# Three graph convolutions at the start of a fused convolution, attention and expert kernel

## The chip, the cores and the metric

The kernel runs on one core of a Trainium2 chip. The time is the device time in microseconds of one execution; three runs of the kernel before took 1002.51 to 1003.75 us, median 1003.73. TensorE is the matrix engine, VectorE (DVE), ScalarE (ACT) and GpSimd (POOL) work on rows, and SyncE (SP) issues the transfers.

## The reference

`x` is 16 x 256 x 16 x 16 (sample, node or channel, feature, time). Three blocks follow one another:

```python
x = x + graph_conv(group_norm(x))        # attention over time (16x16) and over nodes (256x256), 3 Chebyshev
                                         # filters, a convolution over time, residual, relu, norm over time
t = tokens(x)                            # 16 x 256 tokens of 256 channels
t = t + linear_attention(layer_norm(t))  # causal, 16 heads, elu + 1
t = t + moe(layer_norm(t))               # 16 experts of 64, 4 chosen within 2 of 4 groups, and a shared one of 512
```

The convolution of a sample needs only that sample, and so do attention and experts. All is fp32; the large products of attention and experts are made of three products of high and low halves (`mm3`, L501 to L503), and each weight matrix is split into such halves once, at the start.

## The kernel before, in words

The 16 samples go in 8 pairs. Each pair passes five chains of steps: `conv` (22 steps: gn, xg, xT0 ... tc1), `tail` (xb, z1, z2, z3: the norm over time and the sum with x), `attn` (tok0 ... wo1), `route` (tk0 ... cb: layer norm and the choice of experts) and `ffn` (for j from 0 to 11 the steps gu, h, dn, w, on TensorE the gate and up products, the spread product of routed chunks and the down product).

The order of all steps is written out in three texts, OPENING, BODY (used for five turns) and CLOSING. A word such as `1:p2` is step p2 of pair 1, and `+2` puts in the next two steps of the ffn chain, whose own order is fixed. `program()` makes one list of them, and `run` (L504 and on) walks that list on every engine: each engine issues only its own part of a step, in the order of the list. No engine goes ahead of the list; the engines are tied by semaphores, and each chain counts its own results (`Signal`). Up to the first word with a plus, OPENING holds the convolutions of pairs 0 and 1, attention and routing of pair 0, most of the convolution of pair 2 and the first steps of pair 1's attention. In BODY the ffn of pair p, the attention of pair p+1 and the convolution of pair p+2 are laid beside one another.

Products of conv, attn and route go to four PSUM banks in a ring: a tile takes the bank of the fourth tile before it in the order and waits for that one's last reader (`wait_bank`). The steps Y0, Y1, S.., rd take four banks each and p2 two. The ffn has g_ps, u_ps and d_ps, and num serves values and routing.

The scratch of a convolution is a "room". There are two: room 0, for pair 0, lies in the memory that attention uses later (`shared`), and all other pairs use room 1, one after another. Therefore, from pair 2 on, gn and xg of a pair wait for the pair before it (o1, xb1, n30, n31, vs1).

The weights come in 15 pieces of 384 KB (the first is smaller), loaded by SP behind all inputs with no wait (L569) into `raw`, a buffer whose place in memory is that of the low halves (`wqkv_l`, `gate_l`, `up_l`, `down_l`): the high half is written elsewhere by ScalarE (`split`, L661), and then the low half over the raw piece by VectorE (L813). Both splits hang on steps by two tables, HIGH_AT and LOW_AT, such as `"1:st1": 6`, six low splits behind pair 1's st1. The first gu step waits for 6 low halves of weights behind the attention's, gu of j = 2 for all gate and up pieces.

A pair's x is loaded as soon as xb1 of the pair before is done (`prefetch`). POOL does xb, half of z1 and z3, and the low half of the hidden values (L647) in each w step.

Of the lines that are named below: L1218 is gn's product, L1225 the transposes xT, L1237 M, L1191 Y, L1288 sp (with vs_s), L1305 o, L1177 S, L1206 V, L1336 tok and tk, L945 the product with the Chebyshev filters, L950 to L974 the tail, L1031 the causal mask.

Of the kernel before, what the change touches and what calls it, by code (L numbers as in the profile page):

```python
# [54 lines left out]
class Signal:  # L55

    def __init__(self, sem, names, first=None):
# [316 lines left out]

# [1184 lines left out]
```

## Time and profile before

| | us |
|---|---|
| median of three runs | 1003.73 |
| profiled execution, its own time | 1005.99 |
| its span, first to last instruction | 1004.2 |
| TensorE busy | 941.5 (94%) |
| VectorE busy | 606.8 (60%) |
| ScalarE busy | 426.0 (42%) |
| GpSimd busy | 210.2 (21%) |
| mean granted TensorE clock | 0.952 |

The first feed-forward product starts at 188.43 us; pair 0's transposes at the start of attention (tok0) stand at 95.04, its first scores (S00) at 132.92 and its output product (wo0) at 163.96.

### The profile page before, as it was taken

How to read it: one execution, taken by the hardware profiler on the slowest of the kernel's cores; microseconds unless marked ns; L12 is line 12 of the kernel's file. 1: busy time of each engine (PE TensorE's matmuls, PEld its weight loads, DVE VectorE, ACT ScalarE, POOL GpSimd, SP SyncE). 2: the span in 40 equal slices, each digit the busy share in tenths (PEclk: the TensorE clock that was granted, in tenths of full speed). 3: DMA queues.
4: the chain of work that ended last, by engine and by line, in shares of the span. 5: the costliest groups of instructions: out<-in, count | busy, mean ns of one | idle time of the engine just before them, and what ended most of it. 6: DMA issues, size and time to landing. Idle time of an engine off the chain costs nothing.

```text
span 1004.2 us, 20050 instructions
## 1 busy us (share of the span) xinstructions
PE 941.5 (94%) x8208; PEld 832.8 (83%) x8208; DVE 606.8 (60%) x1630; ACT 426.0 (42%) x808; POOL 210.2 (21%) x184
## 2 busy tenths in 40 slices
PE   4797779999999999999999999999999999999997
...
PEclk9689757999999999999999999999999999999999
...
DMA packets 14378, 17.78 MB, mean 18 GB/s; under 512 B 1072, under 2 KB 12720, under 8 KB 14288
## 3 DMA queue, kind: packets, MB, share of 16 engines
...
## 4 chain that ended last, share of the span: by engine, by line
PE 86%; DVE 6%; ACT 6%; issue 1%; POOL 0%; DMA 0%; POOLq 0%; SPq 0%; DVEq 0%; ACTq 0%
PE ring L1305 9%; PE g_ps L501 5%; PE d_ps L501 5%; PE d_ps L503 4%; PE d_ps L502 4%; PE g_ps L503 4%; PE g_ps L502 4%; PE u_ps L501 4%; PE u_ps L502 4%; PE u_ps L503 4%; PE ring L1177 4%; PE num L1206 3%; PE ring L1288 3%; PE ring L501 3%; PE ring L503 3%; PE ring L502 3%
## 5 line engine op out<-in xcount | busy, mean ns | idle before, releaser
L647 POOL TENSOR_TENSOR hl<-hb,hh 128x512 fp32r<-128x512 f32 x96 | 127.2, 1325 | 494.4 <-ACT hh L791 494.4
L1145 DVE TENSOR_TENSOR hb<-sl,u_ps 128x512 f32<-128x512 f32 x88 | 60.2, 684 | 99.9 <-PE u_ps L503 48.4
L791 ACT ACTIVATE hh<-hb 128x512 fp32r<-128x512 f32 x96 | 60.8, 633 | 140.1 <-DVE hb L1149 119.7
L501 PE MATMUL d_ps<-hh,down_h 128*128 128x256 f32 x384 | 114.9, 299 | 1.9 <-POOL hl L647 1.9
L501 PE MATMUL g_ps<-normed_h,gate_h 128*128 128x256 f32 x352 | 109.0, 310 | 3.6 <-DVE scb L1061 3.5
L503 PE MATMUL d_ps<-hh,down_l 128*128 128x256 f32 x384 | 107.5, 280 | 0.0
L502 PE MATMUL d_ps<-hl,down_h 128*128 128x256 f32 x384 | 107.4, 280 | 0.0
L503 PE MATMUL g_ps<-normed_h,gate_l 128*128 128x256 f32 x352 | 100.4, 285 | 0.0
L501 PE MATMUL u_ps<-normed_h,up_h 128*128 128x256 f32 x352 | 100.1, 284 | 0.0
L502 PE MATMUL g_ps<-normed_l,gate_h 128*128 128x256 f32 x352 | 100.1, 284 | 0.0
L502 PE MATMUL u_ps<-normed_l,up_h 128*128 128x256 f32 x352 | 100.1, 284 | 0.0
L503 PE MATMUL u_ps<-normed_h,up_l 128*128 128x256 f32 x352 | 99.9, 284 | 0.0
L1031 DVE TENSOR_TENSOR shared<-ring,constants 128x512 f32<-128x512 f32 x128 | 79.2, 680 | 23.5 <-PE ring L1177 23.5
L788 ACT ACTIVATE sl<-g_ps 128x512 f32<-128x512 f32 x88 | 52.6, 598 | 74.5 <-PE g_ps L503 74.2
L501 PEld LDWEIGHTS d_ps<-hh,down_h 128*128 128x128 f32 x384 | 72.2, 188 | 11.0 <-issue 5.6
L501 PEld LDWEIGHTS g_ps<-normed_h,gate_h 128*128 128x128 f32 x352 | 67.2, 191 | 14.6 <-issue 11.8
L502 PEld LDWEIGHTS d_ps<-hl,down_h 128*128 128x128 f32 x384 | 72.3, 188 | 1.7 <-issue 1.7
L503 PEld LDWEIGHTS d_ps<-hh,down_l 128*128 128x128 f32 x384 | 72.3, 188 | 0.0
L502 PEld LDWEIGHTS g_ps<-normed_l,gate_h 128*128 128x128 f32 x352 | 67.5, 192 | 0.8 <-issue 0.5
L503 PEld LDWEIGHTS g_ps<-normed_h,gate_l 128*128 128x128 f32 x352 | 67.6, 192 | 0.0
L501 PEld LDWEIGHTS u_ps<-normed_h,up_h 128*128 128x128 f32 x352 | 67.4, 191 | 0.0
L502 PEld LDWEIGHTS u_ps<-normed_l,up_h 128*128 128x128 f32 x352 | 67.3, 191 | 0.0
...
## 6 DMA issues: line engine op xcount, KB each, us to landing
out_x<-kept SPq DMA_DIRECT2D x16, 256.0 KB, 2.1
x_s<-in_x SPq DMA_DIRECT2D x14, 256.0 KB, 3.0
raw_weights<-in_gateT SPq DMA_DIRECT2D x4, 384.0 KB, 9.2
raw_weights<-in_upT SPq DMA_DIRECT2D x4, 384.0 KB, 10.1
raw_weights<-in_down SPq DMA_DIRECT2D x4, 384.0 KB, 12.6
cheb_s<-in_cheb SPq DMA_DIRECT2D x3, 256.0 KB, 4.8
raw_weights<-in_wqkvT SPq DMA_DIRECT2D x2, 384.0 KB, 6.9
shared<-in_x SPq DMA_DIRECT2D x2, 256.0 KB, 2.9
```

What stands on the lines that cost most here:

```text
L501: eng.matmul(ps, wh, xh, start=start, stop=False, **how)
L502: eng.matmul(ps, wh, xl, start=False, stop=False, **how)
L503: return eng.matmul(ps, wl, xh, start=False, stop=stop, **how)
L647: pool.tensor_tensor(hl[:, j % 2, :], hb, hh[:, j % 2, :].bitcast(F32), ALU.subtract).then_inc(*ffn_pool.mark(p, f"lo{j}"))
L788: act.activation(sl, gate_up(p, j)[0][:, :], ACT.Silu).then_inc(*ffn_act.mark(p, f"si{j}"))
L791: act.activation(hh[:, j % 2, :], hb, ACT.Copy).then_inc(*ffn_act.mark(p, f"hi{j}"))
L1031: dve.tensor_tensor(p_s[:, j, :].rearrange("p (h l) -> p h l", h=4), tile(p, n)[:, :].rearrange("p (h l) -> p h l", h=4), const_at("causal ...
L1145: dve.tensor_tensor(hb, sl, gate_up(p, j)[1][:, :], ALU.mult).then_inc(*ffn_dve.mark(p, f"h{j}"))
L1177: last = pe.matmul(tile(p, n)[:, 2 * c * P:(2 * c + 2) * P], k_f[rows, c, cols], q_eo[rows, :, c, cols], start=True, stop=True, tile_posit ...
L1206: last = pe.matmul(num[rows, c * L + lc * P:c * L + lc * P + P], v_s[:, b, lc, 4 * c + j, 16 * odd:16 * odd + 32], p_s[:, j, (2 * c + odd) ...
L1288: last = pe.matmul(t[:, kc * N:(kc + 1) * N], vs_s[:, jc, kc * P:(kc + 1) * P], g.th[:, b, jc, :], start=(jc == 0), stop=(jc == 1))
L1305: last = pe.matmul(t[:, c * N:(c + 1) * N], g.y_s[b][:, m, c, k], g.a_s[:, k, m, :], start=(k == 0 and m == 0 and c == 0), stop=(k == 2 an ...
```

## The change

There are three rooms in place of two. Pair 0 keeps room 0, a new room 1 serves pair 1 and lies in `raw`, in the place of gate (second row block), up and down weights, with its small fields in `sl` and `hb`; pairs from 2 on use the room of their own. So pair 2 doesn't wait for pair 1. Its x is loaded right behind pair 1's, ahead of all weights of the convolution.

Because room 1 lies where ten of the pieces are loaded, only five pieces are loaded from the start (the spread rows, wqkv twice, gate's first row block twice). SP then waits for n30 and n31 of pair 1, the end of its tail, before the other ten. The order of pieces changes with that.

The splits become steps of the order (`high0` to `high14`, `low1` to `low14`), and so do 24 fillers, `hot0` to `hot23`, each one matmul of the identity with 256 columns of constants into g_ps, whose result nothing reads. All of the fillers stand ahead of the first ffn step. OPENING is new: gn and xg of all three pairs first, then the three convolutions in turn, with 1:o1, 1:tc0, 1:tc1, pair 1's tail and 2:sp1 to 2:o1 beside attention and routing of pair 0. High5 and low5, the first of the ten late pieces, stand at 0:wo0 and 0:wo1; low7, for which the first gu step now waits, stands behind 1:nrm; high12 to 14 and low10 to 14 stand behind 0:gu0. The steps ahead of 0:gu0 are the same as before but for 1:xl1, which goes behind it, and 0:r1 and 2:xb, which come ahead. BODY is ordered anew with the same steps and the same 50 ffn steps a turn. CLOSING is unchanged.

The order, and the end of `program()`'s input (the lines with a minus are the old order):

```diff
 CHAINS["ffn"] = ffn_steps()
+CHAINS["warm"] = [f"hot{i}" for i in range(24)]
+CHAINS["high"] = [f"high{i}" for i in range(15)]
+CHAINS["low"] = [f"low{i}" for i in range(1, 15)]
+ONCE = ("warm", "high", "low")
+ROOMS = 3
 FIRST = {"conv": "gn", "tail": "xb", "attn": "tok0", "route": "tk0"}
 AHEAD = {"conv": 1, "tail": 1, "attn": 0, "route": 0}
 TURNS = (2, PAIRS - 2)
 
 OPENING = """
-    0:gn 0:xg 1:gn 1:xg 0:xT0 0:M 1:xT0 0:xT1 1:M 0:Y0 0:prod 1:xT1 0:xb 0:Epre 1:Y0 0:Eexp 1:prod 0:Erep 0:lr 1:Epre
-    0:p2 1:Eexp 0:sp0 1:Erep 0:rv0 0:sp1 1:lr 0:st0 0:rv1 0:Y1 1:p2 0:st1 0:o0 0:o1 1:sp0 0:tc0 1:rv0 1:sp1 1:st0
-    0:tc1 1:rv1 0:z1 1:Y1 0:z2 1:st1 1:o0 1:o1 0:z3 1:tc0 1:tc1 1:xb 0:tok0 0:tok1 1:z1 0:nrm 2:gn 0:xl0 2:xg 0:xl1
-    1:z2 2:xT0 0:k0 2:M 2:xT1 0:k1 0:v1 0:q0 0:v0 0:kt 0:q1 1:z3 2:Y0 2:prod 0:dent 0:kv 2:Epre 2:Eexp 0:rd 0:S00
-    2:Erep 0:V00 0:S01 2:lr 0:at0 0:V01 0:S10 2:p2 0:V10 0:S11 2:sp0 2:rv0 0:V11 0:at1 2:sp1 2:st0 0:wo0 0:wo1 2:rv1
-    2:Y1 0:tk0 0:tk1 0:nrm2 2:st1 2:o0 0:xn0 0:xn1 1:tok0 1:tok1 1:nrm 2:o1 0:lg 1:xl0 1:xl1 +1 0:r1 0:r2 1:k0 1:k1 +1
-    1:v1 1:q0 1:v0 0:r3 2:tc0 +1 1:kt 1:q1 +1 0:silu 0:r4 +2 2:tc1 2:xb 1:dent 0:cb +1 1:kv +2 1:rd +2 1:S00 +1 1:V00
-    0:exp +3 1:S01 +3 2:z1 +1 1:at0 1:V01 1:S10 +4 1:V10 1:S11 +1 1:V11 +1 1:at1 +3 2:z2 1:wo0 +2 1:wo1 +2 1:tk0 1:tk1
-    +5 1:nrm2 2:z3 +3 1:xn0 1:xn1 +6 1:exp +1
+    0:gn 0:high0 0:hot0 0:xg 1:gn 2:gn 1:xg 0:hot1 2:xg 0:xT0 0:hot2 1:xT0 0:M 0:xT1 0:hot3 0:xb 0:Y0 0:high1 0:prod
+    1:M 2:xT0 0:high2 0:hot4 1:xT1 0:hot5 0:Epre 0:Eexp 1:Y0 0:Erep 1:prod 2:M 0:lr 2:xT1 0:low1 0:hot6 0:p2 1:Epre
+    1:Eexp 0:hot7 2:Y0 0:hot8 0:hot9 0:sp0 1:Erep 0:high3 0:rv0 1:lr 0:sp1 0:hot10 2:prod 0:st0 0:hot11 0:rv1 1:p2
+    0:low2 0:hot12 0:Y1 0:st1 2:Epre 0:o0 0:high4 2:Eexp 1:sp0 1:rv0 0:o1 1:sp1 1:st0 0:tc0 2:Erep 0:tc1 1:rv1 2:lr
+    0:hot13 0:hot14 0:z1 0:z2 1:Y1 2:p2 1:st1 0:z3 1:o0 2:sp0 0:hot15 0:tok0 0:tok1 0:nrm 2:rv0 1:o1 0:xl0 0:xl1
+    0:low3 2:sp1 2:st0 0:k0 0:k1 0:v1 0:q0 0:v0 0:kt 0:q1 1:tc0 2:rv1 1:xb 0:hot16 0:dent 0:kv 0:hot17 0:rd 0:S00
+    1:tc1 0:V00 1:z1 0:S01 0:at0 0:hot18 0:V01 0:S10 1:z2 0:V10 0:S11 0:hot19 0:V11 1:z3 0:low4 0:at1 2:Y1 0:wo0
+    0:low5 0:wo1 0:hot20 0:high5 0:hot21 0:high6 0:hot22 0:tk0 0:tk1 0:hot23 0:low6 0:nrm2 2:st1 0:high7 2:o0 0:xn0
+    1:tok0 0:xn1 1:tok1 0:high8 1:nrm 0:low7 0:low8 0:high9 2:o1 0:lg 2:xb 0:r1 0:high10 0:high11 0:low9 1:xl0 +1
+    0:low10 0:r2 0:high12 1:xl1 0:low11 +1 2:tc0 +1 0:low12 2:tc1 0:high13 0:r3 0:low13 1:k0 1:k1 0:silu 0:high14 1:v1
+    +2 0:r4 +1 1:q0 +1 1:v0 1:kt 1:q1 0:cb 0:low14 +1 1:dent 1:kv +1 1:rd +2 1:S00 +2 1:V00 2:z1 +2 1:S01 +1 1:at0 +1
+    1:V01 +2 1:S10 +1 1:V10 +7 1:S11 +3 1:V11 2:z2 +3 1:at1 +2 0:exp 1:wo0 +1 2:z3 1:wo1 +2 1:tk0 +2 1:tk1 +2 1:nrm2
+    +4 1:xn0 1:xn1 +1 1:exp
 """
 
 BODY = """
-    tok0 tok1 +1 lg +1 nrm gn xl0 xg +1 xl1 +1 xT0 r1 M xT1 +1 k0 +1 k1 v1 r2 +2 r3 Y0 +1 q0 v0 kt q1 prod silu r4 +2
-    Epre dent cb kv +1 rd +2 Eexp S00 +2 Erep +1 lr +3 p2 +2 sp0 rv0 sp1 +1 st0 V00 +2 rv1 Y1 +3 xb S01 +1 st1 +1 at0
-    +1 o0 +1 o1 V01 +1 S10 +1 tc0 +1 tc1 V10 z1 S11 +1 V11 +2 at1 +1 z2 +1 wo0 +1 wo1 +2 tk0 tk1 +5 nrm2 z3 +1 xn0 xn1
-    exp +1
+    tok0 tok1 +1 lg +1 nrm gn xl0 xg +1 xl1 +1 r1 xT0 M +1 k0 k1 +1 r2 v1 xT1 r3 +2 Y0 q0 v0 kt q1 silu +1 r4 +1 prod
+    +1 cb dent kv +1 Epre +1 rd +2 Eexp Erep +1 lr +2 S00 +2 p2 +2 sp0 rv0 sp1 +1 st0 V00 +1 rv1 +2 Y1 +1 S01 +3 st1
+    at0 o0 xb +1 V01 S10 +1 o1 +1 tc0 tc1 z1 +1 V10 +1 S11 +1 V11 +3 at1 z2 +1 wo0 wo1 +3 tk0 tk1 +4 nrm2 +1 z3 +1 xn0
+    xn1 +1 exp
 """
...
```

Rooms, pieces and the loads:

```diff
         rooms = [conv_room(shared[:, 0:3072], shared[:, 3072:6144], shared[:, 6144:7168], shared[:, 7168:7680], shared[:, 2816:3008]),
+                 conv_room(raw[:, 3072:6144], raw[:, 6144:9216], raw[:, 9216:10240], sl, hb),
                  conv_room(*(sb(n, [P, w])[:, :] for n, w in (("first", 3072), ("filters", 3072), ("x_s", 1024), ("conv_small", 424), ("row_sums", 192))))]
 
         def room(p):
 
-            return rooms[min(p, 1)]
+            return rooms[min(p, ROOMS - 1)]
...
             PIECES.append((wqkvT[c * P:(c + 1) * P, :], wqkv_h[:, c, :], wqkv_l[:, c, :], raw[:, wide * c:wide * (c + 1)]))
-        for part in (slice(wide, 2 * wide), slice(0, wide)):
-            for w, high, low, at in ((gateT, gate_h, gate_l, 2 * wide), (upT, up_h, up_l, 6 * wide)):
-                for k in range(2):
-                    PIECES.append((w[k * P:(k + 1) * P, part], high[:, k, part], low[:, k, part], raw[:, at + k * FF + part.start:at + k * FF + part.stop]))
+
+        def feed_forward(w, high, low, at, k, half):
+            part = slice(half * wide, (half + 1) * wide)
+            PIECES.append((w[k * P:(k + 1) * P, part], high[:, k, part], low[:, k, part], raw[:, at + k * FF + part.start:at + k * FF + part.stop]))
+
+        for half in (1, 0):
+            feed_forward(gateT, gate_h, gate_l, 2 * wide, 0, half)
...
 
-        ONE_PART = 3 + 4
...
         BOTH_PARTS = 3 + 8
         ROUTED_DOWN = {2: 13, 3: 14, 4: 15, 5: 15}
-        HIGH_AT = {"0:xT1": 2, "0:Epre": 2, "0:p2": 2, "1:Epre": 2, "0:rv1": 1, "0:Y1": 2, "1:Y1": 2, "1:o0": 2}
-        LOW_AT = {"0:Erep": 2, "0:p2": 2, "1:p2": 2, "0:st1": 2, "1:st1": 6}
-
-        def splits(p, name, at):
-
-            here = f"{p}:{name}"
-            if here not in at:
-                return []
-            order = [w for w in (f"{q}:{n}" for q, n in PROGRAM) if w in at]
-            before = sum(at[n] for n in order[:order.index(here)])
-            return range(before, before + at[here])
-
-        PREP_POOL = 12
...
             for b in range(2):
-                sp.dma_start(rooms[0].x_s[:, b], x_v[0, b]).then_inc(first_x_loaded, 16)
+                sp.dma_start(rooms[0].x_s[:, b], x_v[0, b]).then_inc(early_x_loaded[0], 16)
             sp.dma_start(cs[:, 0:256], consts[:, 0:256]).then_inc(load["first"], 16)
             sp.dma_start(sm[:, :], small).then_inc(load["small"], 16)
             sp.dma_start(cs[:, 256:], consts[:, 256:]).then_inc(load["rest"], 16)
             for b in range(2):
-                sp.dma_start(rooms[1].x_s[:, b], x_v[1, b]).then_inc(x_loaded, 16)
+                sp.dma_start(rooms[1].x_s[:, b], x_v[1, b]).then_inc(early_x_loaded[1], 16)
+            for b in range(2):
+                sp.dma_start(rooms[2].x_s[:, b], x_v[2, b]).then_inc(x_loaded, 16)
...
             for i in range(len(PIECES)):
+                if i == EARLY_PIECES:
+                    sp.wait_ge(tail_dve.of(1), tail_dve.at(1, "n30"))
+                    sp.wait_ge(tail_pool.of(1), tail_pool.at(1, "n31"))
                 sp.dma_start(PIECES[i][3], PIECES[i][0]).then_inc(piece_loaded[i], 16)
 
             def prefetch(p):
...
```

What the engines do for the new steps, and the waits that now begin with pair 3:

```diff
             def front(p, name):
+                if name in CHAINS["high"]:
+                    split(int(name[4:]))
+                    return
...
+                if name in CHAINS["low"]:
+                    split(int(name[3:]) - 1)
+                    return
...
                 if name == "gn":
-                    dve.wait_ge(x_loaded if p else first_x_loaded, 32 * max(p, 1))
...
                     dve.wait_ge(conv_pool.of(p), conv_pool.at(p, "rstd"))
-                    if p > 1:
...
                     dve.wait_ge(*filled_at(p, name))
-                    if b == 0 and p > 1:
...
+                if name in CHAINS["warm"]:
+
+                    pe.matmul(g_ps[:, 0:N], ident, cs[:, 0:N], start=True, stop=True)
+                    return
...
```

Elsewhere `Signal` gets one semaphore for each of pairs 0 and 1 and one for all from pair 2 on, and the constants that count POOL's first memsets go up by one.

## Rows read from the trace of the kernel before

**Rows 1.** The page: busy time of the engines, then TensorE and its clock in forty slices.
```profile
...
PE 941.5 (94%) x8208; PEld 832.8 (83%) x8208; DVE 606.8 (60%) x1630; ACT 426.0 (42%) x808; POOL 210.2 (21%) x184
...
PE   4797779999999999999999999999999999999997
...
PEclk9689757999999999999999999999999999999999
...
```

**Rows 2.** Windows: length, busy us (instructions) by engine, clock, DMA share, GB/s.
```profile
...
0.00:13.35 13.35, 0.80 (x3) 0.74 (x4) 6.84 (x35) 1.51 (x2) 5.02 (x17) 1.00 0.88 277
13.35:95.04 81.69, 69.36 (x450) 55.30 (x451) 47.41 (x103) 38.24 (x84) 10.23 (x9) 0.81 0.21 73
95.04:132.92 37.88, 24.39 (x174) 18.52 (x173) 29.62 (x84) 15.94 (x34) 6.68 (x6) 0.69 0.01 3
132.92:163.96 31.04, 27.10 (x245) 19.32 (x245) 14.09 (x25) 4.29 (x11) 0.00 (x0) 0.61 0.00 1
163.96:188.43 24.47, 22.84 (x142) 18.46 (x141) 11.71 (x36) 9.63 (x23) 2.02 (x2) 0.93 0.00 1
188.43:208.43 20.00, 20.00 (x147) 18.91 (x146) 16.64 (x63) 13.67 (x24) 3.67 (x3) 1.00 0.08 27
300.00:900.00 600.00, 587.69 (x5335) 525.10 (x5334) 377.76 (x1010) 270.10 (x511) 132.19 (x107) 0.99 0.03 9
...
```

**Rows 3.** Waits of TensorE, 0 to 189 us, then 300 to 900: us, times, longest.
```profile
...
PE ring L1218 <- DVE conv_small L855: 12.6, 2, 6.8
PE ring L1218 <- DVE shared L855: 6.7, 1, 6.7
...
PE g_ps L1466 <- ACT sl L788: 5.1, 6, 1.0
...
```

**Rows 4.** Timeline of TensorE: start, us, instruction: the vs_s product at either clock.
```profile
...
35.44 3.75 PE L1288 MATMUL ring<-shared,vs_s 128*128 128x256 f32 x8 [1.54 <-ACT shared L707]
...
66.41 1.89 PE L1288 MATMUL ring<-first,vs_s 128*128 128x256 f32 x8
...
```

**Rows 5.** Timeline, all engines: first statistics and scaling, pair 0's tail, 1:o1 in part.
```profile
...
10.85 1.40 DVE L846 BATCH_NORM_STATS2 conv_small<-x_s 128x6 f32<-128x256 f32 x4
...
15.44 1.73 DVE L870 TENSOR_SCALAR first<-x_s,conv_small 128x256 f32<-128x256 f32 x4 [1.13 <-POOL conv_small L610]
...
17.07 0.42 DVE L875 TENSOR_TENSOR shared<-ring,small_parameters 128x256 f32<-128x256 f32 x1
...
74.62 1.40 DVE L950 TENSOR_REDUCE shared<-kept 128x32 f32<-128x512 f32 x2
83.70 1.27 POOL L635 TENSOR_TENSOR kept<-kept,shared 128x512 f32<-128x512 f32 x1
85.68 5.34 PE L1305 MATMUL ring<-filters,first 128*128 128x256 f32 x24
...
```

**Rows 6.** Lines L661 and L813, the splits: ns min/median/max, first and last start.
```profile
...
L661 ACT ACTIVATE gate_h<-raw_weights x4: 825/826/827, 24.3 to 49.3; 128x768 fp32r<-128x768 f32 x4
...
L813 DVE TENSOR_TENSOR gate_l<-raw_weights,gate_h x4: 946/949/1473, 35.1 to 63.4; 128x768 fp32r<-128x768 f32 x4
...
```

**Rows 7.** Timeline of VectorE in attention 0's score loop.
```profile
...
135.07 2.48 DVE L1031 TENSOR_TENSOR shared<-ring,constants 128x512 f32<-128x512 f32 x4 [2.36 <-PE ring L1177]
...
155.35 2.48 DVE L1031 TENSOR_TENSOR shared<-ring,constants 128x512 f32<-128x512 f32 x4 [2.63 <-PE ring L1177]
...
```

**Rows 8.** Issues of transfers, 0 to 189 us: KB each, median us to landing.
```profile
...
raw_weights<-in_gateT SPq DMA_DIRECT2D x4, 384.0 KB, 9.2
...
raw_weights<-in_down SPq DMA_DIRECT2D x4, 384.0 KB, 12.6
x_s<-in_x SPq DMA_DIRECT2D x4, 256.0 KB, 3.7
...
x_s<-in_x SPq DMA_DIRECT2D x14, 256.0 KB, 3.0
...
```

**Rows 9.** Timeline of ScalarE behind the first gu step.
```profile
...
194.95 1.28 ACT L788 ACT_TABLE_LOAD   x1
196.25 0.60 ACT L788 ACTIVATE sl<-g_ps 128x512 f32<-128x512 f32 x1
...
```

More of the change, by code:

```diff
@@ L55, with __init__ @@
 class Signal:
-    def __init__(self, sem, names, first=None):
-        self.sem, self.names, self.first = sem, names, first
+    def __init__(self, sem, names, early=()):
+        self.sem, self.names, self.early = sem, names, early
         self.turns = {}
     def of(self, pair):
-        return self.first if self.first is not None and not pair else self.sem
+        return self.early[pair] if pair < len(self.early) else self.sem
     def at(self, pair, name):
-        before = pair - 1 if self.first is not None and pair else pair
+        before = pair - len(self.early) if pair >= len(self.early) else 0
         return before * len(self.names) + self.names.index(name) + 1
@@ L165, in program @@
         put(int(word.split(":")[0]) if ":" in word else None, word.split(":")[-1])
-    names = [n for c in CHAINS for n in CHAINS[c]]
-    assert sorted(out) == sorted((p, n) for p in range(PAIRS) for n in names)
+    every = [(p, n) for p in range(PAIRS) for c in CHAINS if c not in ONCE for n in CHAINS[c]]
+    assert sorted(out) == sorted(every + [(0, n) for c in ONCE for n in CHAINS[c]])
     for c in CHAINS:
+        if c in ONCE:
+            continue
         orders = [[n for q, n in out if q == p and n in CHAINS[c]] for p in range(PAIRS)]
@@ L194 @@
 GROUPS = [f"{b}{lc}" for b in range(2) for lc in range(2)]
-NO_TILE = ["xg", "Eexp", "rv0", "rv1", "nrm", "nrm2", "at0", "at1", "exp", "silu"] + ["V" + g for g in GROUPS] + CHAINS["tail"] + CHAINS["ffn"] + "lg r1 r2 r3 r4 cb".split()
+NO_TILE = ["xg", "Eexp", "rv0", "rv1", "nrm", "nrm2", "at0", "at1", "exp", "silu"] + ["V" + g for g in GROUPS] + CHAINS["tail"] + CHAINS["ffn"] + [n for c in ONCE for n in CHAINS[c]] + "lg r1 r2 r3 r4 cb".split()
 RING = 4
@@ L373, in rows_of, with early @@
             return kept[:, p % 3, :, b, :].rearrange("p m (o t) -> p m o t", t=T)
+        def early(name):
+            return [sem(f"{name}_of_pair{p}") for p in range(ROOMS - 1)]
         load = {n: sem("load_" + n) for n in ("first", "small", "rest", "graph", "blocks")}
         x_loaded = sem("x_loaded")
-        first_x_loaded = sem("first_x_loaded")
+        early_x_loaded = early("x_loaded")
         piece_loaded = [sem(f"piece_loaded{i}") for i in range(15)]
@@ L400, in graph_attention_moe @@
             "M": "um sums left0 right1 left1", "prod": "te", "Epre": "emax esub", "Eexp": "e1 e2 e3 e4 e5 esum erec ET", "Erep": "EW WE", "p2": "pb0 pb1",
-            "sp0": "smax0", "sp1": "smax1", "rv0": "rinv0", "rv1": "rinv1", "st0": "A00 A01 A02", "st1": "A10 A11 A12"}), sem("first_conv_by_dve"))
+            "sp0": "smax0", "sp1": "smax1", "rv0": "rinv0", "rv1": "rinv1", "st0": "A00 A01 A02", "st1": "A10 A11 A12"}), early("conv_by_dve"))
         conv_act = Signal(sem("conv_by_act"), in_order("conv", {
@@ L580, in store @@
                     sp.dma_start(out_v[p, b], x1_at(p)[:, :, b, :]).then_inc(out_stored[p % 3], 16)
-            for p in range(2, PAIRS):
+            for p in range(ROOMS, PAIRS):
                 prefetch(p)
-                if p >= 3:
-                    store(p - 3)
+                store(p - 3)
             for p in range(max(PAIRS - 3, 0), PAIRS):
@@ L669, in front @@
                 if t is not None:
-                    if name == "o0":
-                        for i in splits(p, name, HIGH_AT):
-                            split(i)
                     act_reads = name in ("xT0", "xT1", "lr", "o0", "o1", "tc0", "tc1", "xl0", "xl1", "xn0", "xn1", "kt", "q0", "q1", "k0", "k1", "v0", "v1")
@@ L768, in front @@
                     act.activation(normed_h[p % 2][:, c, :], t[:, :], ACT.Copy).then_inc(*route_act.mark(p, f"hi{c}"))
-                if name != "o0":
-                    for i in splits(p, name, HIGH_AT):
-                        split(i)
             def route(p, name):
```

35 lines of the change are left out of this document (22 added, 13 removed).

## The prediction

> **What bounds the kernel now.** I read the busy line and the forty slices of the page first [rows 1]. TensorE is busy for 941.5 of 1004.2 us. The reader is to see that all of the slack stands at the front: seven slices hold tenths of 4 to 9 with a granted clock of 5 to 9 tenths, and from the eighth on both lines stand at 9. The 600 us from 300 to 900 show 587.7 us of TensorE and a clock of 0.99 [rows 2]: 12.3 us idle, some 2.3 us for each of the five turns of the body. So nothing that leaves TensorE's work as it is can win much behind 188 us, and whatever is won before pair 0's feed-forward network starts (188.43) is carried to the end, because from there on TensorE is full.
>
> Next the windows of the opening [rows 2]. Of 188.43 us, TensorE is busy for 144.5. From the table: idle 43.9, of which 12.6 are the load and the first statistics (0 to 13.35); the waits name them, the two longest being 6.8 and 6.7 us on the sums of the statistics [rows 3]. That leaves 31.3 us of idle time behind 13.35: 12.3 up to pair 0's tok0 (95.04), 13.5 up to its first scores (132.92), 3.9 in the loop of scores and values, 1.6 behind it. The clock is the second loss. A mean of 0.81 over 81.7 us, between the two levels 1.2 and 2.4 GHz, is 31 us at the low one; likewise 23.5, 24.2 and 3.4 us for the next three windows, 82 us together. With the busy shares of those windows (0.85, 0.64, 0.87, 0.93) some 66 us of work ran at half clock. The same eight passes of the vs_s product take 3.75 us at 35.44 and 1.89 us at 66.41 [rows 4], so half of it, 33 us, is lost. The work at full clock is then 144.5 - 33 = 111.5 us. The opening is thus 12.6 start + 111.5 work + 33 clock + 31.3 idle.
>
> **What the change leaves.** Counting the steps of both orders ahead of 0:gu0, the set is the same, but for 1:xl1, which goes behind (about 0.5 us), so the 111.5 us stay. What changes is who lies beside whom. Now pair 2's convolution starts at 100 us and fills attention 0, a chain as slow as itself; after the change three convolutions lie beside one another, pair 1's o1, tc and tail and pair 2's o0 and o1 fill attention 0, and 24 fillers of 128x256 stand at the places where the queue is to have gaps.
>
> **The fillers.** The nearest row is vs_s, four products of the same 128x256 fp32 shape in 1.89 or 3.75 us [rows 4]: 0.47 or 0.94 us each, so 24 cost 11.3 us at full clock and 22.6 at half. In a gap they are free (they write g_ps, idle until 188). The lower bound is below nothing: they raise the activity, and all of the 33 us could come back. I take two thirds of them inside gaps.
>
> **Start to 0:tok0, now 95.04.** On VectorE 2:gn goes ahead of 1:xg and 2:xg ahead of 0:M. One gn is 1.4 us of statistics and about as much of small steps, one xg 1.7 [rows 5]; both stand ahead of 0:M's first product, which is at 17.07 now, and the waits for POOL of 1.1 us are covered. TensorE's 0:xT0 starts at 13.6 now because 1:gn is ahead; it waits for 2:gn then, about 17.6. I put 0:M's product at 21 and 0:prod at 23 (now 21.4), and 0:lr some 3 us late. From there the low splits help: of the fourteen that now stand in VectorE's queue ahead of 0:z3, two are left, 12 x 0.95 = 11.4 us off VectorE [rows 6]. At full clock sp0 and sp1 give back 1.9 us each, so that 0:o0 starts near 51 (now 53.8). Behind 0:o0 the new order has on TensorE 0:o0, 0:o1 and 1:o0 (5.3 each [rows 5]), 1:sp0, 1:sp1 and 2:sp0 (1.9 each), 0:tc0 and tc1 (2.0 each), 1:Y1 and 2:p2 (1.1 each), st (0.5 twice), 2:Erep and 2:lr (1.0 each), three fillers: 32 to 33 us without a gap. The tail of pair 0 goes beside it: from its first sum at 74.62 to POOL's last product start at 83.70 and 1.27 more it is 10.3 us [rows 5], and 11 us of 1:Y1 to 2:sp0 cover it. 51 + 32.5 = 83.5. The walk has no gaps between instructions and no half clock, so I take 87: 8 us gained, as much as pair 1's o1 and two tc (9.2 us) that stood ahead of tok0 and don't now, less what of pair 2 does (8.9 us of TensorE, which fills gaps).
>
> **0:tok0 to 0:S00, now 37.9.** At tok0 nothing but its own normalisation (1.4 + 0.6 + 1.0 + 0.2 + 1.9 us on three engines) is due, and 1:o1 (5.3) covers it; now pair 1's tail lies there on VectorE and TensorE stands 6.8 us [rows 3]. Then xl 1, 2:sp1 1.9, the seven of k, v, q and kt 8.9, the q chain 2.6 with 1:tc0 (2) beside it, dent, kv and rd with their VectorE and ScalarE steps 5: 28 by the walk, 30 taken.
>
> **The score loop, now 31.0.** This is VectorE's round trip: each of four groups is 2.48 us [rows 7], with 0.95 to 2 us of values between, and 0.69 us twice. The change puts 1:z1 (2.6) and 1:z2 (1.3 + 2.8) and 1:z3 (1.4) on VectorE there, and takes 2:p2, sp0 and sp1 (up to 3.78 us each at half clock) out of TensorE's queue. 9.9 + 1.4 + 8.1 + low4's 0.95 is 20.4 us of VectorE and some 6 us of waiting for values: 27, 28 taken. The bounds are 21 (values hidden) and 33 (nothing hidden).
>
> **0:at1 to 0:gu0, now 24.5: the weights.** Ten of fifteen pieces now wait for 1:z3. The first, piece 5, is needed by low5, which stands between 0:wo0 and 0:wo1 on VectorE, so pair 0's second residual and its tk0 wait behind it. A load with an empty queue lands in 3.0 to 3.7 us for 256 KB [rows 8]; the pieces show 9.2 to 12.6 us, but behind one another. With 3.5 us, high5 0.83 and 0.95 for low5 [rows 6], piece 5 is done 5.3 us behind 1:z3; by the order, low4, at1 and wo0 take 4 to 5. So the wait costs 0.5 to 1 us; if a lone piece takes 9.2, it costs 6. I take 1. The ten, 3.9 MB, then take some 14 us at the 277 GB/s of the first window [rows 2]; gu0 needs the first three, and low10 for gu2 comes behind it. The other steps on TensorE: wo 3.5, tk 1, 2:o0 and 2:o1 10.6, xn and 1:tok 2, lg 1.8, 1:xl0 0.5, and fillers that lie in waits: 20.4, with the wait and the edges 23.
>
> Sum: 87 + 30 + 28 + 23 = 168 for 0:gu0, 20.4 us before 188.43. Against the account above: 12.6 + 111 + fillers 13 + clock 16 + idle 15.
>
> **Behind 0:gu0.** VectorE is busy for 16.64 of the 20 us from 188.43 [rows 2]. The change adds low10 to low14 there (4.75 us) and has taken r1 out (1.6): 19.8 of 20. It is the bound there for a while, and TensorE, full now, will stand for some 2 us (0 to 5). 1:k0's exponential goes behind 0:h0's Silu and ahead of 0:h1's, which makes one more table load than now; the row shows 1.28 us with the next activation starting 0.02 us behind its end [rows 9], and ScalarE has 6.3 us free of these 20, so nothing on the path.
> The Trainium skill (ScalarE: Activation LUTs, What ACT_TABLE_LOAD costs) puts a drain of about 1.38 us beside the 1.28 us for each switch. By it the sum would be at most 2.7 us later, by the row at most 1.3; the row, where the next activation starts at once, doesn't show the drain.
>
> **The body.** Its order is new too: xT0 and xT1 later, S00 behind two more feed-forward steps, z1 ahead of dn6. Same work. At best the 12.3 us idle of 600 [rows 2] go, 2 of them likely; the waits that exist are on ScalarE's Silu before the spread product, 1.0 us at most [rows 3], and moving steps can add one per turn: +4. I take 0.
>
> Total: -20.4 + 2 + 0 = -18.4. The profiled execution of before took 1005.99 us for a span of 1004.2; the median of the runs is 1003.73, 2.3 lower. 1003.73 - 18.4 is 985.3, and I say **986**, own range 980 to 992.
>
> **Rivals.**
> *Full clock throughout* (chance 0.18). The page shows the clock falling only in stretches with gaps; if three convolutions and fillers leave none, the 16 us of clock loss in my account shrink to some 5 and 0:gu0 comes at the walk's 159 to 161: about 976. For it: 1.00 where TensorE is 0.93 busy or more. Against: the score loop, where 12 us of full-clock work stands in 27 us, and the first 20 us.
> The Trainium skill (TensorE: Matmul & The Clock Gate, The HAM clock gate) says that the throttled state is the default and that activity releases it. By that rule fillers pay; the windows agree in direction, with 0.61 in the sparse score loop and 1.00 behind 188 us.
> *Attention 0 doesn't shorten* (0.17). Its 93.4 us from tok0 to gu0 are a chain of round trips, and VectorE, which now carries a tail and ten splits beside it, gives nothing: tok0 at 87 as above and 93.4 behind it, gu0 at 180.4, 8 gained, 2 given back behind it: 998; with a slow piece 5 (+5) 1003. For it: VectorE's 2.48 us a group is the same in both orders. Against: in the score loop TensorE's waits now are on pair 2's products at half clock as much as on VectorE.
> *The fillers and pair 2 stand in the way* (0.09), the one on the other side. TensorE's queue is in order; whatever stands ahead of pair 0's chain delays it. Should the clock stay low, 24 x 0.94 = 22.6 us of fillers and the clock loss of 33 us stay, and with 11 us of idle left, 12.6 + 111 + 33 + 22.6 + 11 = 190 for gu0; + 2 behind it and 2 for the body: about 1009. It decides from the point where the idle time removed is less than the fillers' time, 31.3 - 22.6 = 8.7 us left of idle. Against it: fillers are put where the queue is empty, and 31 us of idle are there to take them.
> *The body's order decides* (0.06): 3.7 us more per turn would eat the gain; with 1 to 2 a turn it is 990 to 996.
>
> **How the numbers follow.** Forecast 0.50, the others as above. 972 to 1001 leaves out the slower case, the slow piece and a full-clock case that goes better than its walk, some 0.17 together. A change of 0.2% (2 us) is what measurement can tell. Faster takes the forecast, the full clock, the unshortened chain and most of the body: 0.87; same 0.04; slower 0.09.
>
> **What would show it.** The first g_ps<-normed_h matmul at 168 (161 to 176); 0:tok0's transposes at 87; mean clock of the opening up from 0.78 to 0.88 or so; TensorE idle from 13 us to gu0 down from 31 to about 15; the 24 fillers at 0.47 us mostly; piece 5 landed within 4 us; VectorE over 0.9 busy in the 20 us behind gu0; 1.9 to 2.7 us idle for each 100 us of the body. I am wrong if tok0 comes early and gu0 doesn't (attention chain), if gu0 comes early and the end doesn't (the body), or if low5 waits long (the pieces).

## The result, and the profile after

The changed kernel took 990.38 us by the median of four runs (984.23 to 994.02), the kernel before 1003.74; the ratio is 0.9866, with an interval of 0.9834 to 0.9897. Run again it gave 987.67 (983.71 to 993.83, six runs) and 0.984 [0.9814, 0.9867]. The forecast was 986, with 972 to 1001 as the range. The profiled execution took 994.02 us for a span of 992.2, against 1005.99 and 1004.2: 12.0 us less. It is the longest of the ten executions of its kernel, which matters for the terms below.

The page after, in the same lines as [rows 1]:

```profile
...
PE 940.0 (95%) x8256; PEld 833.1 (84%) x8256; DVE 602.2 (61%) x1630; ACT 427.9 (43%) x810; POOL 210.3 (21%) x185
...
PE   4899879999999999999999999999999999999997
...
PEclk9799978999999999999999999999999999999999
...
```

TensorE's busy time is the same as before, 940.0 and 941.5, although 24 fillers were added. Of the seven slices at the front three hold more work and none less, and the clock is higher in five and lower in none. The windows, cut at the same steps as [rows 2] (first transposes, 0:tok0, 0:S00, 0:wo0, 0:gu0), then two pieces of 20 us behind 0:gu0, then the body:

```profile
...
0.00:17.91 17.91, 3.66 (x11) 2.59 (x12) 10.09 (x53) 2.33 (x3) 6.46 (x20) 1.00 0.93 286
17.91:96.77 78.86, 70.84 (x514) 54.53 (x512) 41.33 (x113) 34.47 (x85) 7.82 (x7) 0.89 0.02 9
96.77:123.60 26.83, 23.89 (x166) 20.43 (x166) 17.88 (x38) 15.37 (x37) 3.23 (x3) 1.00 0.00 1
123.60:149.91 26.31, 19.05 (x254) 14.82 (x254) 19.61 (x39) 2.38 (x5) 4.53 (x4) 0.78 0.04 5
149.91:173.87 23.96, 23.79 (x112) 18.24 (x113) 13.55 (x34) 10.42 (x20) 5.62 (x4) 0.89 0.46 161
173.87:193.87 20.00, 20.00 (x151) 19.01 (x149) 18.69 (x64) 17.08 (x28) 2.50 (x3) 1.00 0.10 29
193.87:213.87 20.00, 18.84 (x207) 16.53 (x206) 16.02 (x27) 10.49 (x19) 4.27 (x5) 1.00 0.00 1
300.00:900.00 600.00, 588.87 (x5378) 526.60 (x5377) 371.98 (x995) 263.98 (x497) 131.14 (x107) 0.99 0.03 9
...
```

Set them against [rows 2] one by one. The start is 17.91 in place of 13.35. Up to tok0 there is nothing gained: 96.77 for 95.04. From tok0 to gu0 it is 77.1 us for 93.4, of it 26.8 for 37.9, 26.3 for 31.0 and 24.0 for 24.5. Gu0 starts at 173.87, 14.6 us earlier. From 300 to 900 TensorE is busy for 588.9 us, before for 587.7.

What is left of TensorE's waits (us in total, times, longest), against [rows 3]:

```profile
...
PE ring L1235 <- DVE shared L870: 6.7, 1, 6.7
PE num L1219 <- DVE shared L1046: 5.9, 3, 2.7
...
```

The longest wait at the start is as it was, and the values of the score loop now wait for VectorE's masks.

### The profile page after: what moved, and what is told of

Read it like the earlier page. It is cut to its first block, busy times and chain, and to the rows that moved or that the text cites. A ratio compares the mean times of both kernels' runs of the same rounds, so it can differ in the third digit from the quotient of the medians.

```text
span 992.2 us, 20146 instructions
## 1 busy us (share of the span) xinstructions
PE 940.0 (95%) x8256; PEld 833.1 (84%) x8256; DVE 602.2 (61%) x1630; ACT 427.9 (43%) x810; POOL 210.3 (21%) x185
## 4 chain that ended last, share of the span: by engine, by line
PE 76%; DVE 5%; ACT 4%; issue 2%; POOL 1%; POOLq 0%; DVEq 0%; ACTq 0%
PE ring L1322 5%; PE g_ps L516 5%; PE d_ps L516 5%; PE g_ps L518 4%; PE u_ps L517 4%; PE g_ps L517 4%; PE u_ps L516 4%; PE d_ps L517 4%; PE d_ps L518 4%; PE u_ps L518 4%; PE ring L1190 3%; PE num L1219 3%; PE ring L1433 3%; PE ring L516 3%; PE ring L518 2%; PE ring L517 2%
## 5 line engine op out<-in xcount | busy, mean ns | idle before, releaser
L516 PE MATMUL d_ps<-hh,down_h 128*128 128x256 f32 x384 | 112.4, 293 | 1.9 <-POOL hl L662 1.9
```

The lines of the kernel that those rows point to most:

```text
L516: eng.matmul(ps, wh, xh, start=start, stop=False, **how)
```

## The experiments

Each kernel below was timed with the kernel before on one chip; a ratio is to that kernel, with its interval.

**The changed kernel once more** (no edit).

> The changed kernel once more, for the spread of its times and to stand beside the others on one chip. The four runs so far lie between 984.2 and 994.0 us, with mean clocks of 0.986 and 0.975. I expect 984 to 994 again, and the time to go with the clock: 1% of clock over 990 us is about 10 us of work at half speed, 5 us of time. If the spread were of the chip and not of the kernel, the kernel before would show it as well (1002.5 to 1005.7 so far).

Measured: 987.67 us, 983.71 to 993.83, ratio 0.984 [0.9814, 0.9867]. Its six executions had a mean clock of 0.976, 0.980, 0.981, 0.984, 0.988 and 0.990 and took 993.8, 988.3, 989.0, 987.0, 984.2 and 983.7 us: time goes with the clock. The kernel before spread less (1001.74 to 1006.1 in 17 runs). The expected range holds, but not the expected price: from 0.976 to 0.990 it is 10.1 us, some 7 us for 0.01 of mean clock and not 5. (By the two levels, 0.01 less is 2% of 990 us at half clock, an estimate of 20 us of work and up to 10 us of time.) What makes the clock differ between executions of one program isn't shown.

**Without fillers.**

```diff
-CHAINS["warm"] = [f"hot{i}" for i in range(24)]
+CHAINS["warm"] = [f"hot{i}" for i in range(0)]
-    0:gn 0:high0 0:hot0 0:xg ...          (and the other 23)
+    0:gn 0:high0 0:xg ...
```

> The changed kernel with all 24 fillers taken out of the order, nothing else. Theory (fillers pay): TensorE's clock in the opening falls from 0.90 towards 0.80, so some 10 to 15 us more of work run at half clock; against it up to 11 us of filler work go, most of which lay in gaps. I expect 3 to 8 us slower than the changed kernel (993 to 998). Rival (fillers stand in the way): 2:Y0 and two fillers stood ahead of 0:sp0 for 4 us at half clock, and 24 of them cost 11 to 22 us; without them the time is 3 to 10 us shorter (980 to 987).

Measured: 998.36 us, 0.9948 [0.9931, 0.9966]. 10.7 us above the changed kernel, more than the 3 to 8 expected, and the rival falls. Windows of the changed kernel, columns as above:

```profile
...
25.00:60.00 35.00, 29.14 (x249) 20.68 (x250) 16.91 (x52) 19.44 (x49) 0.00 (x0) 0.85 0.00 1
123.00:150.00 27.00, 19.14 (x254) 14.95 (x254) 19.61 (x39) 2.92 (x7) 4.53 (x4) 0.78 0.04 5
...
```

and of the kernel without fillers:

```profile
...
25.00:60.00 35.00, 26.17 (x230) 18.82 (x228) 16.91 (x52) 18.82 (x48) 0.00 (x0) 0.76 0.00 1
123.00:150.00 27.00, 18.03 (x237) 14.12 (x241) 19.61 (x39) 2.56 (x6) 4.54 (x4) 0.72 0.03 4
...
```

The clock from 25 to 60 us falls from 0.85 to 0.76 and from 123 to 150 from 0.78 to 0.72, while TensorE is busy for less. These windows show which way the clock goes, and not the 10.7 us: the execution profiled here is the fastest of the kernel without fillers (994.72 us), the other the slowest of the changed kernel (994.02), and their gu0 stand at 174.76 and 173.87. What carries the 10.7 us are the mean clocks of all runs, 0.964 to 0.971 without fillers (994.7 to 1000.9 us) and 0.975 to 0.990 with them (983.7 to 994.0). The order alone is worth 5.5 us (1003.83 - 998.36), the fillers on top of it 10.7.

**The new opening with the old body, and the reverse.** In each, BODY is the text of the other kernel.

> The changed kernel with the BODY text of the kernel before. Theory (all of the gain is the opening): within 2 us of the changed kernel, 988 to 992 by its median. Rival (the body decides): a turn of the new body is worth 1 us or more, so five turns give 5 us or more in one of the two directions: 995 or above if the new body is good, 985 or below if it is bad.

> The kernel before with the BODY text of the changed kernel, the other half of the pair. Theory: 1002 to 1006, as before. Rival (the body decides): 998 or below, or 1009 or above.

Measured: 988.59 us, 0.9828 [0.9803, 0.9854] for the first, and 1004.35, 1.0007 [0.9997, 1.0016] for the second. The body's order is worth nothing that can be measured, in either opening. All of the gain is the opening's.

The first of the two says something more. Its opening is that of the changed kernel, word for word, and its profiled execution took 989.58 us. The same stages, from the start to tok0, the score loop, and from there to gu0:

```profile
...
17.91:99.52 81.61, 73.60 (x514) 56.63 (x512) 41.33 (x113) 34.20 (x84) 7.81 (x7) 0.85 0.02 8
126.36:149.96 23.60, 15.79 (x253) 12.01 (x254) 19.52 (x39) 2.53 (x5) 4.54 (x4) 0.93 0.04 5
149.96:171.30 21.34, 21.17 (x113) 17.28 (x113) 13.54 (x34) 10.27 (x20) 5.62 (x4) 1.00 0.52 181
...
```

With the same order of steps tok0 comes 2.7 us later than in the execution above (99.52 for 96.77), and gu0 2.6 us earlier (171.30 for 173.87). The half clock fell in other places: 0.85 and not 0.89 up to tok0, 0.93 and not 0.78 in the score loop, 1.00 and not 0.89 behind it. The changed kernel's second profile (993.83 us) has tok0 at 96.68 and gu0 at 173.79, like the first. So a stage of one execution carries an uncertainty of some 3 us, and a shift of a milestone by less than that between two kernels shows nothing.

**Fillers in the old opening.** The kernel before, with 24 of the same matmuls where its TensorE stood still:

```diff
-    0:gn 0:xg 1:gn 1:xg 0:xT0 0:M 1:xT0 ...
+    0:gn 0:hot0 0:xg 1:gn 0:hot1 1:xg 0:hot2 0:xT0 0:M 0:hot3 1:xT0 ...   (behind 0:Y0, 0:prod, 1:xT1, 1:Y0, 0:Erep, 0:lr twice,
+                                    0:p2, 0:rv0, 1:lr, 0:rv1, 0:Y1, 0:st1, 1:Y1, 0:z3, 0:tok1, 0:xl0, 0:q1, 0:rd, 0:V00)
```

> The kernel before with 24 fillers of the same kind put into its opening at the places where its TensorE stood still (behind 0:gn, 1:gn, 1:xg and so on to 0:V00), nothing else. Taking the fillers out of the changed kernel cost 10.7 us. Theory (fillers pay by the clock, whatever the order): the opening's clock rises from 0.78 to 0.85 or more and the time falls by 4 to 12 us, 992 to 1000. Rival (they pay only in the new order, which leaves short gaps): 1002 or above.

Measured: 998.35 us (993.54 to 1001.29), 0.9944 [0.9923, 0.9965], 5.2 us below the kernel before. Its windows:

```profile
...
25.00:60.00 35.00, 30.32 (x176) 21.43 (x177) 18.15 (x45) 18.57 (x42) 0.00 (x0) 0.76 0.10 30
96.00:123.00 27.00, 19.05 (x104) 14.37 (x102) 22.54 (x66) 10.80 (x22) 6.70 (x6) 0.81 0.00 1
123.00:150.00 27.00, 19.84 (x254) 14.16 (x254) 16.71 (x35) 6.61 (x18) 0.00 (x0) 0.81 0.01 2
...
```

The same windows of the kernel before:

```profile
...
25.00:60.00 35.00, 27.41 (x129) 20.07 (x130) 16.94 (x39) 17.18 (x40) 0.00 (x0) 0.62 0.11 34
96.00:123.00 27.00, 16.54 (x87) 12.16 (x86) 22.95 (x68) 10.92 (x22) 6.68 (x6) 0.75 0.00 1
123.00:150.00 27.00, 20.85 (x212) 15.16 (x213) 13.96 (x31) 5.55 (x15) 0.00 (x0) 0.56 0.01 1
...
```

The clock from 25 to 60 us rises from 0.62 to 0.76 and in the last window from 0.56 to 0.81. So fillers pay in the old order as well, but half as much. Order alone is 5.5, fillers alone 5.2, both together 16.2, by the medians 5.5 us more than the sum. The intervals of the three ratios reach 1.8 to 2.7 us to either side, so this excess is 5.5 with an uncertainty of some 4, an estimate; and the fillers of the two orders don't stand at the same places.

**Two matmuls in place of one filler** (the line with `pe.matmul(g_ps[:, 0:N], ident, ...)` twice).

> The changed kernel with two matmuls in place of one at each of the 24 places, 48 in all, some 11 us more of filler work at full clock. Theory (the clock of the opening is 0.90 and little is left to win): 2 to 6 us above the changed kernel, 990 to 996. Rival (the clock is still what bounds it): 2 us or more below, 985 or less, with a spread of times smaller than 10 us.

Measured: 991.36 us (985.61 to 991.53), 0.9866 [0.9844, 0.9888], 3.7 above the changed kernel. The intervals touch.

```profile
...
25.00:60.00 35.00, 30.14 (x294) 21.94 (x290) 17.06 (x52) 19.21 (x49) 0.00 (x0) 0.95 0.01 2
123.00:150.00 27.00, 19.86 (x262) 15.37 (x263) 19.52 (x39) 3.62 (x8) 4.53 (x4) 0.87 0.08 19
...
```

The clock is up to 0.95 and 0.87, and the time isn't better: what the clock gives, the work takes. At a mean clock of 0.986 this kernel took 991.4 us and the changed kernel 984.2. So more than 24 don't pay here.

**Only the fillers ahead of 0:tok0, only those behind it.**

```diff
-    ... 0:hot16 0:dent 0:kv 0:hot17 0:rd ...     (and hot18 to hot23)
+    ... 0:dent 0:kv 0:rd ...
```

> The changed kernel with hot0 to hot15 only, those ahead of 0:tok0; the eight behind it are out. Without any filler it took 998.4 us, with all 24 some 988. Theory (each part pays where it stands): the attention of pair 0 runs at a clock of 0.72 in the score loop again, and half of the 10 us is lost: 991 to 995. Rival (only the first sixteen matter): within 2 us of the changed kernel.

> The changed kernel with hot16 to hot23 only, the eight behind 0:tok0. Theory: the three convolutions run at the clock of the kernel without fillers (0.76 from 25 to 60 us against 0.85), and 4 to 7 us are lost: 991 to 995. Rival (only the eight of the attention matter): within 2 us of the changed kernel.

Measured: 992.16, 0.9892 [0.9879, 0.9905] with the sixteen, 992.93, 0.9889 [0.9868, 0.9909] with the eight. The score loop with only the sixteen, then the convolutions with only the eight:

```profile
...
123.00:150.00 27.00, 18.66 (x247) 14.70 (x249) 19.62 (x39) 2.05 (x4) 4.53 (x4) 0.71 0.05 7
...
25.00:60.00 35.00, 26.74 (x201) 17.83 (x200) 16.44 (x52) 17.57 (x45) 0.00 (x0) 0.76 0.00 1
...
```

Each clock falls back to that of the kernel without fillers (0.72 and 0.76) where the fillers are missing. Each part is worth some 5 us where it stands, as both expectations had it.

**Eleven more fillers in what gaps were left.**

```diff
-    0:gn 0:high0 0:hot0 0:xg 1:gn 2:gn ...
+    0:gn 0:hot0 0:hot1 0:hot2 0:hot3 0:high0 0:hot4 0:xg 1:gn 0:hot5 0:hot6 2:gn ...   (1 behind 0:rd, 0:at0, 0:S11, 2 behind 1:z2)
```

> The changed kernel with 11 more fillers at places where its TensorE still stood: four behind 0:gn and two behind 1:gn (4.8 and 2.8 us of waiting at the start), one behind 0:rd (1.4), one behind 0:at0 (1.5), two behind 1:z2 (2.7) and one behind 0:S11 (1.6). Theory (in a gap a filler is free and holds the clock): the first transposes and the score loop run at full clock more often, 2 to 5 us below the changed kernel, 983 to 986, and a smaller spread. Rival (what is left of the clock loss hangs on where the chip's clock looks, not on these gaps): within 1.5 us, as the doubled fillers showed.

Measured: 988.98 us (983.75 to 992.05), 0.9851 [0.9826, 0.9876]: not better than the changed kernel, nor steadier. The rival's numbers hold. This run says nothing on the cause that the rival named.

**Pair 2's convolution behind 0:tok0.**

```diff
-    ... (2:M 2:xT1 2:Y0 2:prod 2:Epre 2:Eexp 2:Erep 2:lr 2:p2 2:sp0 between 1:prod and 0:tok0)
+    ... 0:tok0 0:tok1 0:nrm 2:M 2:xT1 2:Y0 2:prod 2:Epre 2:Eexp 2:Erep 2:lr 2:p2 2:sp0 2:rv0 1:o1 ...
```

> The changed kernel with pair 2's convolution from M to sp0 (ten steps, about 9 us of TensorE) moved from ahead of 0:tok0 to behind 0:nrm; pair 2's gn, xg and xT0 stay, and so do room and fillers. Theory (three convolutions beside one another fill gaps): tok0 comes 3 to 6 us earlier, the stretch from there to 0:gu0 is 8 to 10 us longer, and the time is 2 to 6 us above the changed kernel (990 to 995). Rival (pair 2 stands in the way of pair 0): the time falls by 2 us or more, 986 or below.

Measured: 1008.7 us (1003.76 to 1009.6), 1.004 [1.0023, 1.0058]: 21 us above the changed kernel, far over the 2 to 6 expected. The profiled execution is one of its fastest (1004.03). In TensorE's timeline (start, us, instruction) tok0 comes at

```profile
...
88.91 1.06 PE L1353 MATMUL ring<-constants,kept 128*128 128x128 f32 x8 [1.80 <-DVE kept L998]
...
```

7.9 us earlier. The window from there to the first scores, and the waits in it:

```profile
...
88.91:142.32 53.41, 38.18 (x256) 30.67 (x256) 23.73 (x58) 20.39 (x49) 3.23 (x3) 0.78 0.00 1
...
```

```profile
...
PE ring L1204 <- ACT first L698: 4.9, 1, 4.9
PE ring L1278 <- DVE first L921: 3.2, 1, 3.2
...
```

It takes 53.4 us, 26.6 more than in the changed kernel, for some 9 us of work: the ten steps are a chain of their own, and laid end to end they show their waits and a clock of 0.78. Gu0 is at 187.27. Spread among pairs 0 and 1 they had cost pair 0 only 8 us. With the ten steps in one lump the three rooms and the fillers win nothing against the kernel before. What no run tests is the third way, the ten steps spread beside attention 0 as in the kernel before, so it isn't shown that beside pairs 0 and 1 is the best place for them, only that they must be spread.

**0:sp0 first**, and **pair 0 first.**

```diff
-    0:p2 1:Epre 1:Eexp 0:hot7 2:Y0 0:hot8 0:hot9 0:sp0 1:Erep ...
+    0:p2 1:Epre 1:Eexp 0:hot7 0:sp0 2:Y0 0:hot8 0:hot9 1:Erep ...
```

> The changed kernel with three steps moved: 2:Y0 and the fillers hot8 and hot9, which stand ahead of 0:sp0, go right behind it. In the profile of the changed kernel 0:sp0's input was there at about 42.1 us, and its product started at 46.06, behind 2:Y0 (1.97 us at half clock, and 0.93 us of waiting for a bank) and the two fillers (1.9). Theory (in-order queue: what stands ahead of pair 0's chain delays it): 0:tok0 comes 2 to 4 us earlier and the time falls by 2 to 4 us against the changed kernel, 984 to 986. Rival (it is made good later, since the same work is to be done before tok0 and TensorE is full there): tok0 and the time within 1 us.

```diff
-    ... 2:Y0 0:hot8 0:hot9 0:sp0 1:Erep 0:high3 0:rv0 1:lr 0:sp1 0:hot10 2:prod 0:st0 0:hot11 0:rv1 1:p2
-    0:low2 0:hot12 0:Y1 0:st1 2:Epre 0:o0 0:high4 2:Eexp 1:sp0 1:rv0 0:o1 ...
+    ... 0:sp0 0:rv0 0:sp1 1:Erep 1:lr 0:hot8 0:st0 0:hot9 0:rv1 0:high3 0:Y1 0:hot10 0:st1 0:hot11 0:o0 0:high4
+    0:low2 1:p2 2:Y0 0:hot12 2:prod 2:Epre 2:Eexp 1:sp0 1:rv0 0:o1 ...
```

> The changed kernel with the stretch between 0:p2 and 0:o1 put in another order: sp0, sp1, st0, Y1, st1 and o0 of pair 0 go as early as their inputs allow, and 2:Y0, 2:prod, 2:Epre and 1:p2 go behind 0:o0. Moving 2:Y0 and two fillers alone brought 0:sp0 forward by 4.4 us and 0:o0 not at all, as pair 1's Erep, lr and p2 stood between them. Theory (0:o0 came 8.6 us later than my walk had it because pair 0's own steps stand behind those of pairs 1 and 2): 0:o0 starts near 52 in place of 59.6, 0:tok0 3 to 5 us earlier, and the time is 2 to 4 us below the changed kernel, 983 to 986. Rival (what is taken out ahead of o0 has to be done ahead of tok0 all the same, and leaves TensorE idle and its clock low): 0:o0 comes early, tok0 doesn't, and the time is the same or above, 988 to 992.

Measured: 988.4 us, 0.9855 [0.9836, 0.9874] for the first (the same as the changed kernel), 993.82, 0.9893 [0.9874, 0.9913] for the second (6 us slower). TensorE's timeline of the first, 0:sp0, 2:Y0, 0:o0, 0:tok0:

```profile
...
41.61 1.96 PE L1305 MATMUL ring<-shared,vs_s 128*128 128x256 f32 x8 [0.69 <-ACT shared L722]
46.30 1.15 PE L1204 MATMUL ring<-theta_s,first 32*128 32x96 f32 x32 [2.73 <-ACT shared L727]
...
60.86 7.66 PE L1322 MATMUL ring<-shared 128*128 128x256 f32 x24
...
98.61 1.06 PE L1353 MATMUL ring<-constants,kept 128*128 128x128 f32 x8
...
```

0:sp0 starts 4.4 us earlier, 2:Y0 then waits 2.7 us for the ring, and o0 and tok0 are no earlier: 60.86 and 98.61, between what executions of the unchanged opening show (59.64 and 96.77, 61.96 and 99.52). Of the second, 0:o0, 2:Y0, 0:tok0:

```profile
...
56.54 5.66 PE L1322 MATMUL ring<-shared 128*128 128x256 f32 x24
...
65.66 1.15 PE L1204 MATMUL ring<-theta_s,first 32*128 32x96 f32 x32 [2.40 <-DVE raw_weights L940]
...
103.58 1.07 PE L1353 MATMUL ring<-constants,kept 128*128 128x128 f32 x8
...
```

0:o0 comes 3.1 us earlier than at 59.64, tok0 6.8 us later than at 96.77. Both times the rival was right by the times: what is put behind 0:o0 must be done ahead of tok0 all the same. That its gaps stay open meanwhile is the reading of the second run, not tested apart.

No version was found that beats the changed kernel beyond the intervals.

## Why the prediction was right, and where it wasn't

The direction and the size were right, 13.4 us of the forecast 17.7 by the medians (16.2 when run again) and 14.6 of 20.4 at gu0, and so was the place as between opening and body. Within the opening the place was half wrong: 8 us were to come ahead of tok0, where nothing came, and 12.4 between tok0 and gu0, where 16.3 came. That 986 is so near the 987.7 of the second measurement is in part luck, as errors of opposite sign met. Part by part, from the profiled execution of 994.02 us:

- **Start to 0:tok0: predicted 87, measured 96.8.** This is the step that failed. The prediction walks pair 0's chain and has 0:o0 at 51 and tok0 at 87. 0:o0 was at 59.6, so 8.6 of the 9.8 us were lost ahead of it:

```profile
...
17.91 1.06 PE L1242 MATMUL ring<-constants,shared 128*128 128x128 f32 x4
...
27.78 0.60 PE L1242 MATMUL ring<-constants,raw_weights 128*128 128x128 f32 x4
...
42.40 1.97 PE L1204 MATMUL ring<-theta_s,first 32*128 32x96 f32 x32 [0.93 <-DVE sl L903]
44.31 1.92 PE L1227 MATMUL g_ps<-constants 128*128 128x256 f32 x4
46.06 1.89 PE L1305 MATMUL ring<-shared,vs_s 128*128 128x256 f32 x8
...
59.64 0.79 PE L1322 MATMUL ring<-shared 128*128 128x256 f32 x1
...
```

The first two rows are the same four passes of a transpose, 1.06 and 0.60 us: half clock at the start. 0:sp0 stands behind 2:Y0 and two fillers at half clock, ready at 42 and started at 46. But the last two experiments show that this queueing isn't the cause of the late tok0: with sp0 at 41.6 tok0 was at 98.6, and with o0 at 56.5 it was at 103.6. The account does fit. In the window before, 81.7 us held 69.4 of busy TensorE and 12.3 of idle; after, 78.9 us hold 70.8 and 8.0. The start is 4.6 later, busy time 1.5 more, idle 4.3 less: 1.7 later in all. The clock's gain is an estimate by the prediction's own method: half clock for 31 us before and 17 after, 13.2 and 7.8 us lost, so 5.4 given back. Fourteen of the fillers lie in this window, 6.6 us at the 0.47 each of the forecast, and the rest of the work is nearly the same (9.2 us of pair 1 out, 8.9 of pair 2 in). So the fillers have eaten what the clock gave back. The start came as walked (transposes put at 17.6, product of 0:M at 21, here 17.9 and 20.6); the mis-sized term is the allowance of 3.5 us for gaps and half clock on the way to tok0, where 8.0 us of idle time and some 17 us at half clock (about 8 us of time) were to be paid. Three profiled executions of this opening have tok0 at 96.8, 96.7 and 99.5, none near 87.
- **Tok0 to S00: predicted 30, measured 26.8.** Better: the clock was 1.00 all along, which is 0.69 in [rows 2]. Pair 1's o1 and tc0 lie in it as said.
- **The score loop: predicted 28, measured 26.3**, at a clock of 0.78 with 19.05 us busy. VectorE, busy for 19.6 us, is the bound as said; the waits for its masks are 5.9 us. But TensorE's clock has its part: at 0.93 the same loop took 23.6 us with VectorE busy for 19.5.
- **At1 to gu0: predicted 23, measured 24.0**, and here the pieces were the open term. The first late piece, its issue on SyncE and its high split on ScalarE:

```profile
...
148.08 0.33 SPq L585 DMA_DIRECT2D raw_weights<-in_gateT  x1
...
151.58 0.84 ACT L676 ACTIVATE gate_h<-raw_weights 128x768 fp32r<-128x768 f32 x1 [0.58 <-DMA raw_weights<-in_gateT]
...
```

It was issued at 148.08 and split from 151.58 on: 3.5 us, the value taken, and not the 9.2 of the far bound. On VectorE the first residual, low5, the second residual:

```profile
...
153.72 0.75 DVE L1056 SCALAR_TENSOR_TENSOR kept<-ring,small_parameters,kept 128x512 f32<-128x512 f32 x1 [4.20 <-PE ring L1433]
154.39 0.95 DVE L825 TENSOR_TENSOR gate_l<-raw_weights,gate_h 128x768 fp32r<-128x768 f32 x1
156.24 0.75 DVE L1056 SCALAR_TENSOR_TENSOR kept<-ring,small_parameters,kept 128x512 f32<-128x512 f32 x1 [0.90 <-PE ring L1433]
...
```

VectorE then waits 0.9 us for TensorE, so the wait for piece 5 cost nothing (1 us taken). What was longer is the output product, 6.29 us at half clock in this execution and 3.67 in the profiles of sp0 first and pair 0 first; with it at 3.67 the new opening with the old body took 21.3 us for this stage.
- **Behind gu0: predicted 2 us lost, measured 2.0, by another cause.** The transposes xl of pair 2 at the start of BODY, before and after (the same steps lie ahead of them in both orders):

```profile
...
280.09 1.13 PE L1343 MATMUL ring<-constants,shared 128*128 128x128 f32 x8
...
```

```profile
...
267.53 1.20 PE L1360 MATMUL ring<-constants,shared 128*128 128x128 f32 x8
...
```

They lie 12.56 us apart, the two gu0 14.56. Of the 2.0 us lost, 1.16 are idle time and 0.84 are busy time of TensorE (91.80 for 90.96); 1:xl1, which now lies there, was priced at 0.5, and the rest isn't traced. VectorE was busy for 18.7 of 20 us behind gu0, 19.8 were predicted, and TensorE did not stand in that window at all. The 1.16 us were lost in the next one, behind a table load on ScalarE, which the prediction had priced at nothing on the path; ScalarE's timeline and TensorE's wait:

```profile
...
198.79 1.28 ACT L800 ACT_TABLE_LOAD   x1
200.08 0.60 ACT L800 ACTIVATE sl<-g_ps 128x512 f32<-128x512 f32 x1
...
```

```profile
...
200.82 0.47 PE L1483 MATMUL g_ps<-comb,spread 128*128 128x256 f32 x2 [1.16 <-ACT sl L800]
...
```

The row agrees with [rows 9]: the activation starts 0.01 us behind the load's end, and the drain that the Trainium skill (ScalarE: Activation LUTs, What ACT_TABLE_LOAD costs) puts beside the load doesn't show; what was wrong was the premise that the load is covered, since the activation behind it, 0:h2, is what the spread product waits for. That the two sizes agree is luck.
- **The body: predicted 0, measured 0**, by both exchanges.

Of the rivals, the fillers in the way is refuted (taking them out costs 10.7 us), and so is full clock throughout: doubling the fillers brought the clock to 0.95 and won nothing. By the rule of the Trainium skill (TensorE: Matmul & The Clock Gate, The HAM clock gate) that activity releases the throttle, fillers raise the clock, and the windows with, without and with double fillers agree; but each costs its own time, which the rule leaves out. That attention 0 wouldn't shorten was wrong too: it is 16.3 us shorter, 8.7 of it idle time and 7.6 busy time, although eight fillers were added; how much of the 7.6 is the clock and how much other work isn't told apart. The likeliest case came about, with 9.8 us too many hoped for in its first part and 3.9 too few in the rest up to gu0.
